# FFN columns in three chunks of 392/392/384, and a new order of the stages on every engine

## The reference

```
base_out = einsum('btd,od->bto', x, base_W) + base_b        # 1024 -> 1024
logits   = einsum('btd,nd->btn', x, router_W) + router_b    # 1024 -> 15
probs    = softmax(logits); topk_p, topk_i = top_k(probs, 8)
w        = einsum('btk,btke->bte', topk_p, onehot(expert_map[topk_i]))
h        = einsum('btd,erd->bter', x, A)                    # 1024 -> 8 experts x 16 = 128
out      = base_out + 2 * einsum('bter,eor->bto', h * w, B)
```

## Time and profile before

| | us |
|---|---|
| median of 3 runs (lowest, highest) | 2320.03 (2318.91, 2320.72) |
| span of the profiled execution | 2315.8 |
| PE busy in the span | 2160.1 (93%) |
| DVE busy | 1843.7 (80%) |
| ACT busy | 1527.5 (66%) |
| POOL busy | 1095.6 (47%) |

### The profile page before, as it was taken

One profiled execution on the slowest core, in us unless ns is written; L12 is line 12 of the kernel. 1 busy time (PEld: TensorE's weight loads), 2 busy tenths in 40 slices (PEclk: granted clock), 3 DMA queues, 4 the chain that ended last, 5 costly groups with the idle time before them and its releaser, 6 DMA issues.

```text
span 2315.8 us, 51899 instructions
## 1 busy us (share of the span) xinstructions
PE 2160.1 (93%) x14117; PEld 1805.7 (78%) x14117; DVE 1843.7 (80%) x4980; ACT 1527.5 (66%) x2921; POOL 1095.6 (47%) x1350
## 2 busy tenths in 40 slices
PE   2366999999999999999999999999999999999997
PEld 2245888888888888888888888888888888888776
DVE  8666788888888888888888888888888888887763
ACT  4465676667766677666777667676676766767552
POOL 5543554445544455444554445544455444554321
PEclk8577999999999999999999999999999999999999
DMA  5201111222112221122221222212222112221111
GB/s 150 65 26 36 56 51 47 64 64 64 50 46 64 64 64 58 37 64 64 64 61 35 64 64 64 63 34 61 64 64 64 35 60 64 64 64 38 62 40 34
DMA packets 90061, 132.61 MB, mean 57 GB/s; under 512 B 20379, under 2 KB 63559, under 8 KB 90006
## 3 DMA queue, kind: packets, MB, share of 16 engines
q1 hardware_dynamic: 87496, 126.12, 18.4%
q10 hardware_dynamic: 2510, 5.83, 0.8%
HBM read 55.17 MB, written 76.74 MB: 57 GB/s over the span
## 4 chain that ended last, share of the span: by engine, by line
issue 44%; PE 27%; POOL 9%; DVE 7%; ACT 6%; POOLq 1%; DVEq 0%; ACTq 0%
PE bank L1644 5%; PE bank L1545 5%; POOL CB L934 4%; PE bank L1600 3%; PE bank L1575 2%; DVE NF L1274 2%; ACT L1039 2%; POOL XD L885 2%; PE bank L1718 2%; PE bank L1702 2%; POOL RS L919 1%; PE bank L1577 1%; PE bank L1576 1%; POOL RS L898 1%; PE bank L1692 1%
## 5 line engine op out<-in xcount | busy, mean ns | idle before, releaser
L1545 PE MATMUL bank<-w_hi,XHI 128*128 128x512 f32 (+1 forms) x1560 | 623.0, 399 | 0.0
L1545 PE MATMUL bank<-w_lo,XHI 128*128 128x512 f32 (+1 forms) x1560 | 555.1, 356 | 0.0
L1545 PE MATMUL bank<-w_hi,XLO 128*128 128x512 f32 (+1 forms) x1560 | 554.6, 355 | 0.0
L1180 DVE SCALAR_TENSOR_TENSOR CX<-bank,cw,CX 128x252 f32<-128x252 f32 (+5 forms) x804 | 335.6, 459 | 62.2 <-ACT CX L977 62.0
L934 POOL TENSOR_TENSOR CB<-CB,CM 48x252 f32<-48x252 f32 (+5 forms) x402 | 293.1, 729 | 153.5 <-ACT CM L962 142.6
L1545 PEld LDWEIGHTS bank<-w_hi,XLO 128*128 128x128 f32 x1560 | 295.5, 189 | 46.9
L1545 PEld LDWEIGHTS bank<-w_lo,XHI 128*128 128x128 f32 x1560 | 297.0, 190 | 41.2
L1545 PEld LDWEIGHTS bank<-w_hi,XHI 128*128 128x128 f32 x1560 | 296.7, 190 | 41.2
L962 ACT ACTIVATE T<-bank 64x512 f32<-64x512 f32 x256 | 151.4, 591 | 261.9 <-PE bank L1634 257.2
L898 POOL TENSOR_TENSOR RS<-VE,half_neg 128x1 f32<-128x1 f32 x65 | 35.5, 546 | 370.7 <-DVE VE L1372 370.7
L925 POOL TENSOR_TENSOR RB<-m_gt,AS 128x512 fp32r<-128x512 f32 x134 | 165.0, 1231 | 56.9 <-DVE AS L1446 56.9
(11 more groups left out here) (295 smaller groups left out, 5375.1 us busy)
## 6 DMA issues: line engine op xcount, KB each, us to landing
carried<-T SPq DMA_DIRECT2D x65, 512.0 KB, 4.7
T<-carried SPq DMA_DIRECT2D x65, 512.0 KB, 3.8
out<-HB SPq DMA_DIRECT2D x129, 256.0 KB, 3.2
tables<-tab SPq DMA_DIRECT2D x8, 560.0 KB, 4.1
TB<-tables SPq DMA_DIRECT2D x64, 70.0 KB, 2.7
carried<-U SPq DMA_DIRECT2D x65, 64.0 KB, 3.5
XM<-carried SPq DMA_DIRECT2D x65, 64.0 KB, 4.7
XI<-in_x SPq DMA_DIRECT2D x128, 32.0 KB, 2.7
```

What stands on the lines that cost most here:

```text
L1180: inc(STT(CX[:, c, :, s:CS], src[:, :, 0:CS - s], cw[:, c, k:k + 1], CX[:, c, :, s:CS], ALU.mult, ALU.add), "conv")
L1545: ins = mm(bank[:, 0:c1 - c0], xs_[:, 1 - p, k, :], ws[:, k, c0:c1], start=(c0 == HID and k == 0 and n == 0), stop=(last == k and n == 2))
```

## The change

The 1168 columns are cut at 392 and 784: two chunks of 392 base columns go to `bO[0]` and `bO[1]`, and `bR` takes 384 columns: the last 240 base columns, 128 adapter, 15 router, 1 padding. The bias of the 240 columns is added by one more matmul in `route(0, 1)`. A third `lora(2)` of 240 columns overwrites the front of `bR`; so that nothing is lost, DVE first adds the 240 base columns to `HB` in a new step `add_base`, and `final` has a third part. The lists of calls of PE, DVE, ACT and POOL are put into a new order; SP waits for `fin=4` instead of 2. The diff, cut to its core:

```diff
+    C1, C2 = 392, 784
+    HC = HID - C2
...
-        bO = banks[0:2]
+        bO = banks[0:3]
         bR = banks[2]
...
-                   rt=1, sm=NSM, se=1, hw=1, trh=1, hwe=1, hwl=1, o=2, fin=2)
+                   rt=1, sm=NSM, se=1, hw=1, trh=1, hwe=1, hwl=1, o=3, fin=4)
...
                     def final(h):
                         if E:
                             wait(dve, te, o=h + 1)
+                            if h == 2:
+                                wait(dve, te, fin=1)
+                            c = slice(SPLIT[h], SPLIT[h + 1])
+                            inc(TT(HB[:, 1 - p, c], bO[h][:, 0:SPLIT[h + 1] - SPLIT[h]], HB[:, 1 - p, c], ALU.add), "fin")
+                    def add_base():
+                        if E:
+                            wait(dve, te, rt=1)
+                            inc(TT(HB[:, 1 - p, C2:HID], bR[:, 0:HC], HB[:, 1 - p, C2:HID], ALU.add), "fin")
...
                     def route(a, b):
                         if E:
                             if a == 0:
                                 wait(pe, te, xlo=2)
-                                wait(pe, te - 1, hwl=1)
-                            ins = ffn(HID, FW, bR, range(a, b), last=KC - 1)
+                                wait(pe, te - 1, hwl=1, fin=4)
+                            ins = ffn(C2, FW, bR, range(a, b))
+                            if a == 0:
+                                mm(bR[:, 0:HC], row_sel[:, :], base_bias[:, C2:HID], start=False, stop=False)
...
-                            wait(pe, te, hw=1)
-                            inc(tr(bR[:, 256:256 + P], HW[:, :], ident[:, :]), "trh")
+                            wait(pe, te, hw=1, fin=1)
+                            inc(tr(bR[:, HT], HW[:, :], ident[:, :]), "trh")
```

More of the change, by code:

```diff
@@ L698, in build @@
         HW = sb("HW", [P, P])
-        bO = banks[0:2]
+        bO = banks[0:3]
         bR = banks[2]
+        SPLIT = (0, C1, C2, HID)
+        RH, RL = HC, HC + P
+        HT = slice(HC + FW - HID, HC + FW - HID + P)
         bK = banks[3]
@@ L817, in store @@
                 def store(t, p):
-                    wait(sp, t, fin=2)
+                    wait(sp, t, fin=4)
                     apart(sp)
@@ L1425, in split_lo @@
                             wait(dve, td, xhi=g + 1)
-                            wait(dve, td - 2, o=2)
+                            wait(dve, td - 2, o=3)
                             ks = slice(4 * g, 4 * g + 4)
@@ L1450, in final @@
                             wait(dve, te, o=h + 1)
-                            c = slice(HALF * h, HALF * (h + 1))
-                            inc(TT(HB[:, 1 - p, c], bO[h][:, :], HB[:, 1 - p, c], ALU.add), "fin")
-                    kernel_p()
+                            if h == 2:
[6 more added lines that the diff above has]
+                            inc(TT(HB[:, 1 - p, C2:HID], bR[:, 0:HC], HB[:, 1 - p, C2:HID], ALU.add), "fin")
                     gram(0)
                     gram(1)
+                    kernel_p()
                     kernel_sum()
@@ L1465, in body @@
                     times_z()
+                    gated_a()
                     mean_square()
@@ L1471, in body @@
                     conv(3, 0)
-                    conv(3, 1)
[L1473 to L1480, removed]
+                    stats_1(0)
+                    router(0)
+                    router(1)
+                    stats_1(1)
+                    layer_out()
+                    router(2)
@@ L1481, in body @@
+                    gated_b()
+                    add_base()
+                    router(3)
+                    stats_1(2)
+                    stats_1(3)
+                    gated_lo()
+                    router(4)
+                    conv(3, 1)
+                    router(5)
+                    router(6)
+                    shift_1()
                     conv(4, 0)
[L1482 to L1485, removed]
+                    residual(0)
@@ L1486, in body @@
+                    softplus(0)
                     conv(4, 1)
+                    softplus(1)
                     conv(5, 0)
[L1488 to L1497, removed]
                     stats_2(0)
                     residual(1)
+                    softplus(2)
@@ L1500, in body @@
+                    stats_2(1)
+                    router(7)
+                    stats_2(2)
+                    softplus(3)
                     softplus(4)
-                    stats_2(1)
+                    stats_2(3)
+                    router(8)
                     softplus(5)
                     softplus(6)
-                    conv(5, 1)
-                    stats_2(2)
                     softplus(7)
                     softplus(8)
-                    router(8)
                     softplus(9)
+                    shift_2()
@@ L1510, in body @@
                     softplus(10)
                     softplus(11)
-                    stats_2(3)
-                    conv(6, 0)
+                    weighted_lo()
+                    conv(5, 1)
                     softplus(12)
-                    shift_2()
-                    conv(6, 1)
                     split_decays(0)
-                    weighted_lo()
                     split_decays(1)
                     decays_forth(0)
+                    conv(6, 0)
+                    conv(6, 1)
@@ L1521, in body @@
+                    final(0)
+                    split_lo(0)
+                    final(1)
+                    final(2)
                     decays_forth(1)
-                    split_lo(0)
-                    final(0)
-                    final(1)
                     split_lo(1)
@@ L1545, in ffn @@
                                 ins = mm(bank[:, 0:c1 - c0], xs_[:, 1 - p, k, :], ws[:, k, c0:c1],
-                                         start=(c0 == HID and k == 0 and n == 0), stop=(last == k and n == 2))
+                                         start=(c0 == C2 and k == 0 and n == 0), stop=(c0 == C2 and k == KC - 1 and n == 2))
                         return ins
@@ L1573, in lora @@
                             wait(pe, te, hwl=1)
[L1574 to L1577, removed]
+                            c = slice(SPLIT[h], SPLIT[h + 1])
+                            o = bO[h][:, 0:SPLIT[h + 1] - SPLIT[h]]
+                            mm(o, HWS[:, 0, :], lb_hi[:, c], start=(h == 2), stop=False)
+                            mm(o, HWS[:, 1, :], lb_hi[:, c], start=False, stop=False)
+                            inc(mm(o, HWS[:, 0, :], lb_lo[:, c], start=False, stop=True), "o")
                     def up(h):
```

89 lines of the change are left out of this document (45 added, 44 removed).

## The result

The changed kernel takes 2252.61 us (median of 4 runs, 2251.16 to 2257.96) against 2319.47 us for the kernel before (median of 4): a ratio of 0.9719, 95% interval 0.9706 to 0.9733. The prediction was 2244 us in 2212 to 2292. It moved the way that was forecast, by 67 us where 76 were expected. The profiled execution has a span of 2252.1 us, 63.7 us less than before.

A forecast was written before the change was run, and what follows sets the result against it. PE was taken as the bound, with DVE ending level; 1.24 us from chunks plus 0.48 from removed waits less 0.55 for new ones saves 1.17 us a pass, times 65 is 76 us: 2244 us, range 2212 to 2292.

The forecast's parts named there:

- The price per matmul: FFN matmuls on PE: 392 columns cost 0.177 us, 384 cost 0.173; the new cut saves 1.24 us a pass.
- The rival by which the cut saves nothing: FFN matmuls on PE: fixed part plus per-column part, so equal cost for either cut; 2290 to 2320 us, chance 0.05.
- Whatever it streams: Matmuls on PE: each costs 0.11 us whatever it streams, up to 256 columns.
- Nothing to be won from waits: PE, busy 198.77 of 200 us, works without a hole, so waits alone offer no gain.
- The order on PE: Late starts of project_bc and the first lora go, 0.48 us of 0.55 counted; new waits cost 0.55 us a pass.
- step (a): project_out on PE waits for ACT's keep_y, about 0.3 us a pass.
- Step (c): turn_h on PE, behind router(8), starts late by 0.05 to 0.2 us.
- step (b): up(1) on PE needs residual(0), with conv(4,0) and shift_1 in front of it: 0.1 us late.
- Steps (d) and (e): On PE, grams waits for ACT's silu_bc(1), 0.1 us; project_x behind POOL's XD and add_skip, 0.05 us.
- The switches: float32r runs after float32 stages on PE start 0.1 to 0.2 us slower; 12 places before and after, so cancels.
- end together with PE at 31.05 us: DVE's list: 27.65 us busy plus waits gives 31.05 us a pass, level with PE's 30.89, blocking further gain.
- the third rival: DVE and POOL block each other in three more side-by-side pairs; two colliding lose 1.7 us, 2365 us; chance 0.07.

The follow-up runs named there:

- e7_456: e5_keep_y with the columns cut at 456/456/256 instead of 392/392/384; 2255.9 us, one run.
- e8_484: e5_keep_y with the columns cut at 484/484/200 instead of 392/392/384; 2296.9 us, one run.
- e5_keep_y: The changed kernel with ACT's keep_y moved between keep_h(1, 0) and keep_h(1, 1), stats_1(j) waiting for 3 + j keep_h; 2226.44 us, ratio 0.9604.
- e9_dve_order: e5_keep_y with two DVE steps moved: gated_b ahead of router(2), router(8) right behind router(7); 2209.51 us, ratio 0.9531.
- e6_no_conv6: The changed kernel without the convolution's last tap, conv(6, 0) and conv(6, 1), on DVE (output incomplete); 2251.09 us, ratio 0.971.

## Why the prediction came out as it did

**The price per matmul: right.** 0.177 and 0.173 us were taken for 392 and 384 columns, and these runs read 0.177 and 0.173; e7_456 and e8_484 show the same line at 456 and 484, and the floor at 200. The rival by which the cut saves nothing fell with them: 256 columns cost 0.118 us here, hardly more than the 0.1125 of 144. The Trainium skill, "TensorE: Matmul & The Clock Gate", section "Back-to-back issue gap", gives a sustained 81 ns at 128 columns and 131 ns at 512; the straight line that the prediction drew between these two does not hold for this format.

"Whatever it streams" was too wide, though. The floor belongs to runs in which every matmul has weights of 128 by 128 (the `128*128` of the lines): the eight with `16*64` in the earlier trace rows took 0.45 us together, with 64 columns each, where eight with `128*128` took 0.88 with 4 columns. It is also a pace and not a price of each matmul: in the kernel before, the first 144-column matmul behind 512-column ones is followed after 0.07 us, and the 512-column one behind such a run after 0.28 in place of 0.233, which gives it back. What sets the pace is open: no run kept the columns and changed the weights. In the earlier trace rows's run the weight loads (PEld) start 0.11 us apart as well.

**Nothing to be won from waits: wrong.** The prediction read this from 198.77 busy us of 200. The changed kernel is busy for 199.02, and e5_keep_y and e9_dve_order still took some 40 us out of its waits. The records of PE overlap, so a late start shows as idle time only as far as it is longer than the overlap: `project_out` is 0.31 us late, yet from the end of its forerunner's record (1037.78 + 0.34) to its start there are 0.14 us. Late starts have to be read from start to start.

**The order on PE: right in kind, too small in size.** `lora`'s late start went, and the new wait came where step (a) put it, at `project_out` behind `keep_y`. It was sized at 0.3 us; it is 0.31, and 0.10 in the second matmul behind it. Such a 0.10 was taken off where a wait goes away (0.48 for 0.55), but it goes away with the wait and comes with one, so it belongs on top in both places. e5_keep_y gives the worth of this wait: 26 us. Step (c), `turn_h`, came to 0.16 us with what follows it, inside its 0.05 to 0.2. `project_bc`, which was to have no late start, kept 0.15 of its 0.35. These two are what e9_dve_order gave back: 30.73 to 30.41 us a pass. Of step (b) there is 0.05: the first matmul of `up(1)` takes 0.34 us for 0.23 in every second pass. Steps (d) and (e) left no late start. `turn_y`, with 0.05, was not on the list. The five terms of the list add up to 0.60 to 0.75, and 0.55 was taken for them without a reason.

**The switches: they cancel, as the prediction had it.** The prediction let the slow starts of float32r runs behind float32 stages cancel, 12 for 12. One might suspect that a wide first matmul pays more there than a narrow one. The kernel before, from the first FFN matmul behind `s4d(0)` to the first behind `project_x`:

```profile
1024.89 0.42 PE L1545 MATMUL bank<-w_hi,XHI 128*128 128x144 f32 x1
...
1026.09 0.42 PE L1545 MATMUL bank<-w_hi,XHI 128*128 128x144 f32 x1
```

The changed kernel, the same stretch, and `project_z` (L1696), behind which another float32 stage comes:

```profile
1031.81 0.53 PE L1560 MATMUL bank<-w_hi,XHI 128*128 128x384 f32 x1
1032.17 0.34 PE L1560 MATMUL bank<-w_lo,XHI 128*128 128x384 f32 x1
...
1032.52 1.02 PE L1678 MATMUL bank<-U,wx 128*128 128x256 f32 x4
1033.19 0.53 PE L1560 MATMUL bank<-w_hi,XHI 128*128 128x384 f32 x1
...
1045.10 1.03 PE L1696 MATMUL bank<-wz,U 128*128 128x256 f32 x4
1045.96 0.27 PE L1629 MATMUL bank<-ident,H 128*128 128x128 f32 x1
```

The stretch takes 1.20 us before and 1.38 now. Three FFN matmuls and the four of `project_x` lie in it; the wider chunk accounts for 3 x (0.173 - 0.1125) = 0.18 of it, all of the difference. The slow start itself is a matter of where the records part: the first 384-column matmul takes 0.36 us, 0.19 over its own cost, but the four float32 matmuls of `project_x` ahead of such a start take 0.67, where the four of `project_z` take 0.86.

**DVE: wrong, without harm to the number.** I had it end together with PE at 31.05 us and wrote that what PE could have below 30.9 us a pass was not to be had. e6_no_conv6 shows that DVE has room, and e9_dve_order runs below it: (2317.19 - 2209.51) / 65 = 1.66 us off 32.06 make 30.4. The step that failed is its busy time: 27.65 us were summed, 170.08 / 200 x 31.14 = 26.5 were measured. The pairs of the third rival are the larger part of the reason. Groups of DVE of the changed kernel (count, then busy us and mean ns of one): RF, NF, the sum of NF, and the two steps of VB.

```profile
L1439 DVE TENSOR_TENSOR RF<-m_lt,AS 128x512 fp32r<-128x512 f32 x134 | 97.8, 730 | 0.0
...
L1237 DVE TENSOR_TENSOR VB<-VB,V 128x512 f32<-128x512 f32 x64 | 85.3, 1333 | 10.0 <-POOL V L858 3.4
...
L1285 DVE TENSOR_TENSOR NF<-NF,NB 128x512 f32<-128x512 f32 x67 | 63.1, 941 | 7.2 <-POOL NB L882 5.0
L1279 DVE TENSOR_TENSOR NF<-GF,sp_dt 128x512 f32<-128x512 f32 x67 | 47.4, 707 | 0.2
L1231 DVE TENSOR_TENSOR VB<-TB 128x512 f32<-128x512 f32 x64 | 44.4, 694 | 5.6 <-PEq L137 5.6
```

The same groups of the kernel before:

```profile
L1434 DVE TENSOR_TENSOR RF<-m_lt,AS 128x512 fp32r<-128x512 f32 x134 | 142.8, 1104 | 0.0
L1274 DVE TENSOR_TENSOR NF<-GF,sp_dt 128x512 f32<-128x512 f32 x67 | 98.2, 1465 | 0.2
...
L1280 DVE TENSOR_TENSOR NF<-NF,NB 128x512 f32<-128x512 f32 x67 | 77.7, 1160 | 7.2 <-POOL NB L877 5.0
L1226 DVE TENSOR_TENSOR VB<-TB 128x512 f32<-128x512 f32 x64 | 68.5, 1071 | 5.8 <-PEq L135 5.8
L1232 DVE TENSOR_TENSOR VB<-VB,V 128x512 f32<-128x512 f32 x64 | 43.8, 684 | 3.6 <-POOL V L853 3.4
```

In a pass these six (RF runs twice) took 2 x 1.10 + 1.47 + 1.16 + 1.07 + 0.68 = 6.6 us before and take 2 x 0.73 + 0.71 + 0.94 + 0.69 + 1.33 = 5.1 now. The rival had the pairs collide more; they collide less. 1.5 us went, and I had only weighed that it might grow. For one pair the traces show where: before, `gram_forth` ran beside POOL's `gram_back` in each pass from 500 to 2000 us and took 1.53 us; now `gram_back` has ended before it and it takes 0.68, while `kernel_sum`, which now runs beside `gram_back`, went from 0.68 to 1.35. For RF the lists suggest a cause: `carry_h` now stands between the two `decays_back`, and `final` and `split_lo` between the two `decays_forth`. That was not tried on its own.

**Sum.** Taken: 1.24 + 0.48 - 0.55 = 1.17 us a pass. Found, as means over the passes from 500 to 2000 us: 1.13 for the chunks (24 x (0.578 - 0.5305), with medians of 0.178 and 0.1745, less 0.01 for `lora` and the bias) and 0.56 for the two late starts of the earlier trace rows (0.36 and 0.20), less 0.41 at `project_out`, 0.16 at `turn_h`, 0.05 each at `up(1)` and `turn_y`, and 0.06 that is spread over the openings of other stages: 0.96, as between the mean passes of 32.09 and 31.13. So the forecast was too kind by 0.1 us in the chunks, by a few thousandths of a microsecond in each of 24 matmul triples, and by 0.1 us in what starts late. Both are small beside the range. The profiled span came out 12 us over the forecast of 2239.8 and the median 9 over 2244: the 4.2 us that the median stood over that span before are 0.5 here, which is luck.

## What to carry to other kernels

Look for the width below which a run of matmuls no longer gets cheaper, here about 256 columns with weights of 128 by 128, and cut the columns so that no chunk lies under it; but price every place to which the slices then move, since on an engine with its own list a slice is also the cover of somebody's latency. A cut and an order belong together: either alone made this kernel slower by 0.85%. And when one engine is full, follow its largest late start to the step that it waits for, and move that step up: here three such moves, one on ACT and two on DVE, were worth some 40 us.

## What the runs showed that was not expected

A matmul that was waited for costs more than the wait: `project_out`'s four records took 1.13 us after a wait and 1.03 without one, in the changed kernel and in e5_keep_y. Waiting is not the only thing that does this: the four of the first `s4d` product, behind the 64-column matmuls of `mix`, take 1.13 us in the changed kernel too, where the trace lists no wait. What it is was not tried.

The time from start to start cannot be put down to one matmul where the number format changes: behind float32 matmuls the first float32r one seems 0.19 us dear, and the last float32 one just as much too cheap. And a PE that is busy for 199 us of 200 still had 40 us of late starts in its 2250.
